# Attention and experts in one block, the gate multiplication ahead of the Gelus, and four buffers for its result

## The reference, cut to what matters

```python
x = x + tanh(g_xattn) * xattn(layernorm(x), ctx, ctx, w_q, ..., b_o)   # 16 heads, 32 sequences of 128 tokens
x = x + tanh(g_ffn)   * ffn(layernorm(x), W1, b1, W2, b2, Wr, br)

def ffn(x, W1, b1, W2, b2, Wr, br):        # E = 8 experts, D = 256, H = 1024, 4096 tokens
    logits = xf @ Wr + br
    weights = softmax(where(logits >= second_largest(logits), logits, -inf))
    h = gelu(einsum('td,edh->eth', xf, W1) + b1[:, None, :])
    expert_out = einsum('eth,ehd->etd', h, W2) + b2[:, None, :]
    return einsum('etd,te->td', expert_out, weights)
```

## Time and profile before

| what | value |
|---|---|
| median of 3 runs | 860.46 us (858.18 to 860.63) |
| the profiled execution's own time | 861.33 us |
| its span, first to last instruction | 859.6 us |
| mean granted TensorE clock | 0.968 |
| PE busy | 768.7 us (89%) |
| DVE, ACT, POOL busy | 581.4, 480.2, 349.0 us |

### The profile page before, as it was taken

The page is one execution under the profiler, slowest core; times in us unless marked ns, Lnnn a source line. Parts: engine busy times, 40 slices in busy tenths (PEclk is TensorE's granted clock), DMA queues, the critical chain, the costliest instruction groups (busy, mean ns, idle before and its releaser), DMA issues. The chain is left out here.

```text
span 859.6 us, 27596 instructions
## 1 busy us (share of the span) xinstructions
PE 768.7 (89%) x8684; PEld 715.9 (83%) x8685; DVE 581.4 (68%) x1457; ACT 480.2 (56%) x1205; POOL 349.0 (41%) x390
## 2 busy tenths in 40 slices
PE   5499999999999999999827988999999999999992
PEld 3389889888898898888716987999999999999992
DVE  2358999989989999999863535655555555555551
ACT  2156566655656665556514536766666666666661
POOL 2234565555656555566540213333322233232222
PEclk9799999999999999999957999999999999999997
DMA  8876987777888888898245994543444333332222
GB/s 187 155 140 124 186 171 132 147 163 161 151 186 191 189 191 201 212 210 190 89 165 96 232 245 78 72 54 53 57 61 53 53 52 54 58 49 32 27 27 28
DMA packets 124028, 105.84 MB, mean 123 GB/s; under 512 B 60928, under 2 KB 117632, under 8 KB 121728
## 3 DMA queue, kind: packets, MB, share of 16 engines
q1 hardware_dynamic: 110032, 85.51, 46.9%
q0 software_dynamic: 13296, 18.23, 14.0%
q10 hardware_dynamic: 576, 0.56, 0.2%
HBM read 36.54 MB, written 32.19 MB: 80 GB/s over the span
## 5 line engine op out<-in xcount | busy, mean ns | idle before, releaser
L1290 ACT ACTIVATE hf<-bank,b1t,gscale 128x128 f32<-128x128 f32 x568 | 206.5, 468 | 130.3 <-PE bank L1412 127.9
L1265 POOL DMA_INDIRECT out_rows<-yg,gates x71 | 110.9, 1562 | 294.4 <-ACT yg L1299 229.4
L1412 PE MATMUL bank<-xh,wts 128*128 128x128 f16 x3408 | 204.1, 220 | 15.2 <-issue 15.2
L1412 PEld LDWEIGHTS bank<-xh,wts 128*128 x3408 | 198.4, 99 | 16.8 <-issue 15.2
L1426 PE MATMUL bank<-wts,hh 128*128 x1704 | 198.0, 273 | 6.0 <-DVE hh L1321 4.7
L1426 PEld LDWEIGHTS bank<-wts,hh 128*128 128x128 f16 x1704 | 163.5, 98 | 24.8 <-issue 7.1
L1320 DVE TENSOR_SCALAR hh<-hf,hscale 128x512 f16<-128x512 f32 x142 | 69.2, 487 | 168.0 <-ACT hf L1290 162.1
L540 POOL TENSOR_SCALAR_AFFINE_SELECT xh<-rowmax 128x512 bf16<-128x512 bf16 x128 | 93.7, 732 | 133.6 <-DVE rowmax L792 121.1
L1044 PE MATMUL bank<-va,probs 128*128 128x102 f32 x1024 | 138.9, 277 | 8.6 <-DVE ao L740 8.6
L1044 PEld LDWEIGHTS bank<-va,probs 128*128 128x128 f32 x1024 | 125.5, 192 | 11.6 <-DVE ao L740 6.2
L1321 DVE SCALAR_TENSOR_TENSOR hh<-hf,hscale,hh 128x512 f16<-128x512 f32 x142 | 106.7, 751 | 5.1
(11 more groups left out here) (169 smaller groups left out, 975.2 us busy)
## 6 DMA issues: line engine op xcount, KB each, us to landing
wts<-in_W SPq DMA_DIRECT2D x16, 1024.0 KB, 6.5
wts<-keys SPq DMA_DIRECT2D x96, 128.0 KB
wts<-queries SPq DMA_DIRECT2D x96, 128.0 KB
split_weights<-wts SPq DMA_DIRECT2D x8, 1024.0 KB, 5.1
wts<-split_weights SPq DMA_DIRECT2D x8, 1024.0 KB, 7.4
xin<-in_x SPq DMA_DIRECT2D x16, 256.0 KB, 2.8
cin<-in_ctx_in SPq DMA_DIRECT2D x16, 256.0 KB, 3.3
out_rows<-x SPq DMA_DIRECT2D x16, 256.0 KB
```

The lines of the kernel that those rows point to most:

```text
L1265: pool.indirect_dma_start(out=out[:, :], out_offset=bass.IndirectOffsetOnAxis(ap=numbers, axis=0), in_=yg[m % 2][:, :], in_offset=None, co ...
L1290: last = act.activation(hf[b][:, c, :], HB[2 * b + half][:, c % 4 * TILE:(c % 4 + 1) * TILE], ACT.Gelu, bias=b1t[:, bass.ds(e, 1), c], sca ...
L1412: last = pe.matmul(HB[2 * b + half][:, c % 4 * TILE:(c % 4 + 1) * TILE], weight(expert[1], first_at(wp, k, c), P), xh[(m + 1) % RING][:, x ...
```

## The change

Both parts run in one block, so the drain, the meeting of the engines and the jump between them go. What they kept apart is now kept apart by semaphores: SP waits for `scales_ready` before it loads tile 0's rows and for `act_left` (raised by ACT's last one-element Gelu) before it loads `b2`; PE, ACT and DVE wait for `scales_ready` before the experts' program. On ACT the gate multiplication of tile i-1 stands ahead of the Gelus of tile i+1 in the order of the program, where it stood behind them; `yg` has four buffers, so it waits for the scatter of tile i-5, not i-3. The first part's semaphores are now made by the caller, and three of the second part's get new names. All lines inside the two blocks move one level to the left; without that the diff is:

```diff
+        act_left = sem("act_left")
...
-        attention_and_routing(nc, env)
-        experts(nc, env)
+        with nc.Block() as block:
+            attention_and_routing(nc, env, block)
+            experts(nc, env, block)
...
-def attention_and_routing(nc, env):
+def attention_and_routing(nc, env, block):
...
-        def sem(name):
-            return stack.enter_context(nc.semaphore(name))
+        sem = env["sem"]
...
-        with nc.Block() as block:
-
...
             sp.wait_ge(env["rows_placed"], 1)
+            sp.wait_ge(env["scales_ready"], 1)
             load_rows(sp, env, env["tile_row"][0:1, 0:1], env["first_xh"][0], env["gates"][0], 0)
...
-            act.activation(ex[:, 0, 0:1], lgs[:, 0, 0:1], ACT.Gelu)
+            act.activation(ex[:, 0, 0:1], lgs[:, 0, 0:1], ACT.Gelu).then_inc(env["act_left"], 1)
...
-def experts(nc, env):
+def experts(nc, env, block):
...
-        yg = [sb(f"yg{i}", [P, D]) for i in range(2)]
+        yg = [sb(f"yg{i}", [P, D]) for i in range(4)]
...
-        dve_steps, pool_steps, waits_taken = sem("dve_steps"), sem("pool_steps"), sem("waits_taken")
+        dve_steps, pool_steps, waits_taken = sem("e_dve_steps"), sem("e_pool_steps"), sem("e_waits_taken")
...
-        with nc.Block() as block:
-
...
+            sp.wait_ge(act_left, 1)
             sp.dma_start(b2_all[:, :, :].rearrange("p e d -> p (e d)"), b2.partition_broadcast(P)).then_inc(b2_in, 16)
...
-                        in_=yg[m % 2][:, :], in_offset=None, compute_op=ALU.add).then_inc(added, 16)
+                        in_=yg[m % 4][:, :], in_offset=None, compute_op=ALU.add).then_inc(added, 16)
...
             def it(i, m, there):
+                if there(-1):
+
+                    e, p = expert_of(act, i - 1), (m - 1) % 4
+                    act.wait_ge(yb_ready, i)
+                    when(act, before(i, 5), added, added_value(i - 5))
+                    act.activation(yg[p][:, :], yb[p % 2][:, :], ACT.Copy,
+                                   scale=gates[(m - 1) % RING][:, bass.ds(e, 1)]).then_inc(yg_ready, 1)
                 if there(1):
...
-                if there(-1):
-
-                    e, p = expert_of(act, i - 1), (m - 1) % 2
-                    act.wait_ge(yb_ready, i)
-                    when(act, before(i, 3), added, added_value(i - 3))
-                    act.activation(yg[p][:, :], yb[p][:, :], ACT.Copy,
-                                   scale=gates[(m - 1) % RING][:, bass.ds(e, 1)]).then_inc(yg_ready, 1)

+            act.wait_ge(scales_ready, 1)
             all_tiles(act, it)
...
+            dve.wait_ge(scales_ready, 1)
             pipeline(dve, it, 0, MAIN_TILES)
...
+            pe.wait_ge(scales_ready, 1)
             all_tiles(pe, it)
```

More of the change, by code:

```diff
@@ L1163, in experts @@
              "wscale", "wsquares", "padrow", "b1t", "all_slots", "gscale", "hscale", "yscale",
-             "mostint", "tile_no", "tile_expert", "tile_row", "weights_in", "first_xh", "gates"))
+             "mostint", "tile_no", "tile_expert", "tile_row", "weights_in", "scales_ready", "act_left", "first_xh", "gates"))
     with ExitStack() as stack:
@@ new lines, in _, with it @@
+        @block.sync
+        def _(sp):
+            def it(i, m, there):
+                if there(AHEAD) and not (isinstance(i, int) and i + AHEAD == 0):
+                    j, k = i + AHEAD, (m + AHEAD) % RING
+                    when(sp, before(j, RING), added, added_value(j - RING))
+                    settled(sp)
+                    load_rows(sp, env, tile_row[0:1, bass.ds(j, 1)], xh[k], gates[k], k)
+                if isinstance(i, int) and 0 <= i < E - EARLY:
+                    sp.wait_ge(weights_in, 16 * 2 * (EARLY + i))
+                    load_weights(sp, wts, w_dram, EARLY + i, weights_in)
+            sp.wait_ge(act_left, 1)
+            sp.dma_start(b2_all[:, :, :].rearrange("p e d -> p (e d)"), b2.partition_broadcast(P)).then_inc(b2_in, 16)
+            all_tiles(sp, it)
+            sp.wait_ge(weights_in, 16 * 2 * E)
+            sp.wait_ge(b2_in, 16)
@@ new lines, in _, with it, last @@
+        @block.gpsimd
+        def _(pool):
+            def it(i, m, there):
+                if there(0):
+                    pool.wait_ge(yg_ready, i + 1)
+                    when(pool, before(i, 1), added, added_value(i - 1))
+                    settled(pool)
+                    numbers = gates[m][:, E:E + 1].bitcast(I32)
+                    pool.indirect_dma_start(
+                        out=out[:, :], out_offset=bass.IndirectOffsetOnAxis(ap=numbers, axis=0),
+                        in_=yg[m % 4][:, :], in_offset=None, compute_op=ALU.add).then_inc(added, 16)
+            def last(tiles):
+                pool.wait_ge(added, added_value(tiles - 1))
+            pipeline(pool, it, 0, MAIN_TILES)
+            last(MAIN_TILES)
+            ties = pool.value_load(mostint[0:1, 0:1], min_val=0, max_val=E)
+            with pool.If(ties > 2):
+                pipeline(pool, it, MAIN_TILES, ALL_TILES)
+                last(ALL_TILES)
@@ new lines, in _, with it @@
+        @block.scalar
+        def _(act):
+            def it(i, m, there):
+                if there(-1):
[4 more added lines that the diff above has]
+                                   scale=gates[(m - 1) % RING][:, bass.ds(e, 1)]).then_inc(yg_ready, 1)
+                if there(1):
+                    e = expert_of(act, i + 1)
+                    b = (m + 1) % 2
+                    for half in range(2):
+                        act.wait_ge(h_psum, (i + 1) * 2 + half + 1)
+                        when(act, before(i + 1, 2), split_ready, (i - 1) * 2 + half + 1)
+                        for c in range(4 * half, 4 * half + 4):
+                            last = act.activation(
+                                hf[b][:, c, :], HB[2 * b + half][:, c % 4 * TILE:(c % 4 + 1) * TILE],
+                                ACT.Gelu, bias=b1t[:, bass.ds(e, 1), c], scale=gscale[:, bass.ds(e, 1)])
+                        last.then_inc(gelu_ready, 1)
+            act.wait_ge(scales_ready, 1)
+            all_tiles(act, it)
@@ new lines, in _, with it @@
+        @block.vector
+        def _(dve):
+            step = Links(dve, dve_steps)
+            def it(i, m, there):
+                if there(1):
+                    e = expert_of(dve, i + 1)
+                    b = (m + 1) % 2
+                    for half in range(2):
+                        c = slice(4 * half, 4 * half + 4)
+                        dve.wait_ge(gelu_ready, (i + 1) * 2 + half + 1)
+                        when(dve, half == 0 and before(i + 1, 2), y_psum, i)
+                        high = hh[b][:, 0, c, :].rearrange("p c t -> p (c t)")
+                        full = hf[b][:, c, :].rearrange("p c t -> p (c t)")
+                        step(dve.tensor_scalar(high, full, hscale[:, bass.ds(e, 1)], None, ALU.mult))
+                        dve.scalar_tensor_tensor(out=hh[b][:, 1, c, :].rearrange("p c t -> p (c t)"), in0=full,
+                                                 scalar=hscale[:, bass.ds(e, 1)], in1=high,
+                                                 op0=ALU.mult, op1=ALU.subtract).then_inc(split_ready, 1)
+                if there(0):
+                    e = expert_of(dve, i)
+                    if isinstance(i, int) and i == 0:
+                        dve.wait_ge(b2_in, 16)
+                    dve.wait_ge(y_psum, i + 1)
+                    when(dve, before(i, 2), yg_ready, i - 1)
+                    dve.scalar_tensor_tensor(out=yb[m % 2][:, :], in0=YB[m % 2][:, 0:D],
+                                             scalar=yscale[:, bass.ds(e, 1)],
+                                             in1=b2_all[:, bass.ds(e, 1), :].rearrange("p a d -> p (a d)"),
+                                             op0=ALU.mult, op1=ALU.add).then_inc(yb_ready, 1)
@@ new lines, in _ @@
+            settled(dve)
+            step.restart()
+            dve.wait_ge(scales_ready, 1)
+            pipeline(dve, it, 0, MAIN_TILES)
+            ties = dve.value_load(mostint[0:1, 0:1], min_val=0, max_val=E)
+            with dve.If(ties > 2):
+                for lo in range(MAIN_TILES, ALL_TILES, MAIN_TILES):
+                    step(dve.tensor_scalar(tile_no[:, :], tile_no[:, :], float(MAIN_TILES), None, ALU.add))
+                    rows_of_tiles(dve, step, table, lo, min(lo + MAIN_TILES, ALL_TILES))
+                dve.sem_inc(rest_ready, 1)
+                step.restart()
+                pipeline(dve, it, MAIN_TILES, ALL_TILES)
```

1472 lines of the change are left out of this document (693 added, 779 removed).

## The result

The changed kernel took 881.12 us in the median of four runs (880.53 to 882.07), against 860.55 us for the kernel before measured beside it. The ratio on record is 1.0213, 95% interval 1.0174 to 1.0252 (the two medians alone would give 1.0239): slower, as forecast, and inside the range of 866 to 882, but 6 us above the forecast of 875. The profiled execution took 881.0 us with a span of 879.2, so 19.7 us more than that of before (861.33 and 859.6).

What follows compares the result with a forecast made beforehand. PE alone was taken to set the experts' pace, 5.30 us a tile. Round +26.2, late `yb`s +1.8, buffers -6.8, seam -2.8 and tail -3.9 gave +14.5 on the 860.5 median: 875.0 us, range 866 to 882.

Steps and rivals of the forecast that it cites:

- The main term: Experts' tiles: multiplication, Gelus, split and `yb` close one round per tile, 5.68 us against PE's 5.30; +26.2 us.
- The late `yb`s: In 5 places `yb` has unexplained idle time ahead of it, formerly hidden by PE's pace; +1.8 us.
- The buffers: Weight loads: four buffers end ACT's waits for scatters and the PE stalls that follow; -6.8 us.
- the cover that I called thin: Weight loads: the landing at 506.89 serves tile 7's multiplication, due at 506.2; without that cover the 6.8 us stay.
- the rival in which scatters hold ACT: Weight loads: gate multiplications still wait for scatters, now directly ahead of the Gelus; 882 us, chance 0.06.
- The seam: Between the two parts: tile 0's rows load earlier, so PE starts 3.3 us earlier, less 0.5 for tile 1; -2.8 us.
- tile 1's wait for its rows: At the seam: tile 1's rows queue behind `b2` and come only 2.2 us earlier; 0.5 us charged.
- the half clock of the first tile: At the seam: PE starts at 1.2 GHz as before, 0.50 over its first 5 us.
- The tail: At the end: scatter 69 no longer waits for scatter 68, starting 1.7 us after tile 69's `yb`; -3.9 us.
- POOL's answer to the multiplication: After each gate multiplication: POOL starts its scatter within some 0.6 us, so 1.7 us after `yb`.
- One sign: Experts' stretch: PE busy about 93%, with some 0.4 us idle per tile before the second product.
- The rival of the port: Each round: POOL's scatter locks out DVE's split from 3.0 to 3.3 us, 21 us in all; 896 us, chance 0.02.

Runs made afterwards that it cites:

- e1: Changed kernel with the gate multiplication back behind the Gelus (one block, four buffers kept): 855.2 us, ratio 0.9922 to the kernel before.
- e3: Kernel before, still two blocks, with the gate multiplication ahead of the Gelus and four buffers: 881.8 us, ratio 1.0205.
- e5: Changed kernel with the gate multiplication of tile i-1 between the two halves of the Gelus of tile i+1: 854.35 us, ratio 0.9875 to the kernel before.
- e9: Changed kernel with the expert number of tile i+1 read ahead of the gate multiplication instead of behind it: 857.86 us, ratio 0.9928 to the kernel before.
- e10: Changed kernel with a spare DVE operation between the split and `yb`: 891.84 us, ratio 1.0329 to the kernel before.
- e7: Changed kernel with a second, spare multiplication on ACT ahead of each gate multiplication: 884.39 us, ratio 1.0235 to the kernel before.
- e2: Kernel before with four buffers for `yg` instead of two, two blocks and old order kept: 857.41 us, ratio 0.9924.
- e12: Changed kernel with two buffers for `yg` instead of four: 889.2 us, ratio 1.0304 to the kernel before.

## Why the prediction was right, point by point

**The main term** was the closed round, 26.2 us from 5.68 against 5.30. Links and sum came within 0.02 us each, e1 and e3 show that it belongs to the order alone, and e5 and e9 remove it by shortening the round while the order of multiplication and last Gelus stays. Four changes of its length give four times in line:

| run | mean round us | 69 rounds, against after | time, against after (881.12) |
|---|---|---|---|
| e10 | 5.864 | +9.5 | +10.7 |
| e7 | 5.773 | +3.2 | +3.3 |
| e9 | 5.387 | -23.5 | -23.3 |
| e5 | 5.327 | -27.6 | -26.8 |

(e5 and e9 keep the tail of the change. e5's round is PE's pace and no longer that of ACT and DVE.) The times also hold the seam, 1.5 to 2.1 us shorter in these four than in after, and the end of the first part, which differs by some us; that they agree with the rounds to about 1 us is in part luck.

**The late `yb`s** were charged 1.8 us. 395.2 - 69 x 5.67 = 4.0 is what the changed kernel lost besides its links. The trace gives it link by link. Late `yb`s make 1.8 us, nearly all in 7 rounds, just as charged. Another 1.8 us are Gelus that start late behind their multiplication, in 6 rounds, after 1.02 to 1.15 us in place of 0.75; this is one of them, its multiplication at 515.08:

```profile
515.08 0.51 ACT L1286 ACTIVATE yg<-yb,gates 128x256 f32<-128x256 f32 x1 [2.03 <-DVE yb L1331]
516.23 2.90 ACT L1296 ACTIVATE hf<-bank,b1t,gscale 128x128 f32<-128x128 f32 x8 [0.64 <-issue]
```

One late split has 0.35. The prediction had no term for late Gelus, and what makes them late stays open.

**The buffers** were put at 6.8 and gave 5.6 (e2). In the changed kernel no round was lost to scatters: the cover that I called thin held. With two buffers (e12) the same order costs 8 us more by the median and 3.7 us by the rounds of its trace; the rival in which scatters hold ACT had 7 (882 against 875).

**The seam** was put at -2.8 and gave -0.5 in the profile of after, but 2.0 to 2.6 us in the nine other profiles that have one block and `b2` first (16.3 to 16.9 us against 18.9). The step that was too short is tile 1's wait for its rows, charged at 0.5: it is 2.11 us in after, 1.84 in e1 and 0.67 to 1.50 in the other eight. What set after apart from these nine is the clock. These are the stretches around that pause, by the granted clock (the third number from the end), the pause itself and the matmuls behind it in after, and then the matmuls in e1:

```profile
459.30:461.20 1.90, 0.00 (x0) 0.00 (x1) 1.61 (x3) 1.47 (x4) 0.00 (x0) 1.00 0.43 65
461.30:463.30 2.00, 2.00 (x22) 2.00 (x22) 0.75 (x1) 0.00 (x0) 0.00 (x0) 0.53 0.37 70
```
```profile
462.10:464.10 2.00, 2.00 (x38) 2.00 (x38) 1.00 (x2) 0.41 (x2) 0.00 (x0) 1.00 0.34 69
```

In after the clock had risen to 2.4 GHz near the end of tile 0's product (0.84 from 457.7 to 458.7) and stayed there while PE stood. It fell to 1.2 GHz just after PE went on (0.73 from 461.2 to 461.7, 0.50 from there to 464.2), so that tile 1's 48 matmuls took 4.47 us; in e1 they ran at 2.4 GHz and took 2.84, as in the other eight. I had carried over the half clock of the first tile only.

**The tail** was put at -3.9 and gave -3.3 in after, -2.5 in e5 against e1. Scatter 69 starts 1.95 us after tile 69's `yb` (863.96 to 865.91) in place of 1.7: POOL's answer to the multiplication was taken 0.2 us too short.

**Where the 6 us lie.** Between the two profiled executions the sum was to be +14.5 and came to +19.7. Of the missing 5.2, the seam has 2.3, the rounds 1.5 (395.2 against 69 x 5.68 + 1.8 = 393.7, late Gelus above all), the tail 0.6, and 0.7 is the later end of the first part in that execution, which is chance. Medians add 0.9. So no step of the main term failed; the seam's tile 1, its wait and its clock, was mis-sized most. One sign came otherwise than said: PE is busy 96% of the stretch and not 93%, and idle 0.2 us before a second product and not 0.4, since recorded products overlap and hide part of a pause, as shown above.

**The rival of the port** fell for this kernel's time. These are the durations of the split's first operation (minimum, median, maximum) in after, which answer to the earlier trace rows, and then in e5:

```profile
L1320 DVE TENSOR_SCALAR hh<-hf,hscale x142: 479/486/674, 459.3 to 862.6; 128x512 f16<-128x512 f32 x142
```
```profile
L1326 DVE TENSOR_SCALAR hh<-hf,hscale x142: 485/486/826, 463.7 to 837.7; 128x512 f16<-128x512 f32 x142
```

In after 61 of the 142 operations overlap a scatter, which in the steady rounds has some 0.6 us left when the operation starts, as scatters start 1.95 us after `yb` and not 1.7; only 3 of the 61 took over 0.52 us. In e5 it is otherwise: 30 of the 59 operations that overlap a scatter took 0.53 to 0.83 us, half of them 0.72 or more, and none of the other 83 did. So the delay exists beside a scatter, up to 0.34 us; e5's time does not show it, as its round is PE's. What decides when it comes was not tested: the operation starts at other points of the scatter in e5 than in after.
The Trainium skill ("SBUF — State Buffer", section "Who interferes with whom") would have the later of the two wait for the other's whole instruction, if the split's operation runs in a two-port mode, which no run here shows. That would be some 0.6 us of the scatter's 1.62 in after; what the runs show is at most 0.34 us (826 ns in e5), and mostly nothing in after.

## What to carry to other kernels

When an operation that waits is moved ahead of others on an in-order engine, follow what stands behind it until the chain comes back to the same wait, and add the links from start to start. If the chain closes within one iteration, its length is a pace of its own, however idle the engines look; compare it with the pace of the engine that sets the time now. Here the loss could be taken back in two ways that do not undo the move: a register read placed ahead of the wait (23.5 of the 27.9 us that the rounds of after have over those of e1), or the moved operation put one half later (27.6 of them), which makes the kernel 1.25% faster than before. Undoing the move alone gives 0.8%, and the runs do not tell the two apart.

## What the runs showed of the hardware that was not expected

- Reading an expert number into a register between two ACT operations kept the second from starting for 0.74 us after the first; with the number read before, it started after 0.42 (e9). The profile puts only 0.24 us of this down to "issue"; the rest stands inside the multiplication's recorded 0.51.
- From start to start the spare operations took less than their recorded duration: 0.41 us in place of 0.51 on ACT (e7), 0.34 in place of 0.42 on DVE, of which only 0.16 was added to the round's link (e10).
- PE's granted clock fell to half right behind a pause of 2.11 us that came just after it had risen (after). Behind pauses of 0.67 to 1.84 us at the same place it did not (tile 1's product took 2.84 us in nine other profiles), nor behind the pause of 2.10 us in the weight loads of the kernel before, where the whole stretch stands at 1.00. Why it fell in the one case stays open.
- The split's first operation was longer beside some of POOL's scatters only: 30 of 59 in e5 (0.53 to 0.83 us in place of 0.49), 3 of 61 in after.
